# One common table in place of two: where the two attention phases of a decoder and recurrence kernel put their matrix products

## The reference, cut to what matters

```python
def attention(q, k, v, mask):                       # 16 heads of 32 channels
    scores = einsum('bhqd,bhkd->bhqk', q, k) / sqrt(32)
    scores = scores * mask - 10000.0 * (1.0 - mask)
    probs = softmax(scores, axis=-1)
    return einsum('bhqk,bhkd->bhqd', probs, v)

qkv = layernorm(hidden, ln1_s, ln1_b) @ w_qkv + b_qkv          # self attention
x = hidden + merge(attention(split(q), split(k), split(v), ltor_mask)) @ w_ao + b_ao
q = layernorm(x, ln2_s, ln2_b) @ w_q + b_q                     # cross attention
k, v = split2(encoder @ w_kv + b_kv)
x = x + merge(attention(split(q), split(k), split(v), cross_mask)) @ w_co + b_co
x = x + gelu(layernorm(x, ln3_s, ln3_b) @ w1 + b1) @ w2 + b2   # then the recurrent layer
```

## Time and profile before

| | us |
|---|---|
| median of 3 runs | 4188.12 |
| lowest and highest | 4186.58, 4194.16 |
| the profiled execution | 4188.12 |
| its span, first to last instruction | 4186.3 |
| scores of the self phase, first to last | 48.8 to 756.9 |
| scores of the cross phase, first to last | 824.6 to 1555.9 |

### The profile page before, as it was taken

One profiled execution on the slowest core, in us unless ns is written; L12 is line 12 of the kernel. 1 busy time (PEld: TensorE's weight loads), 2 busy tenths in 40 slices (PEclk: granted clock), 3 DMA queues, 4 the chain that ended last, 5 costly groups with the idle time before them and its releaser, 6 DMA issues. The chain is left out here.

```text
span 4186.3 us, 71343 instructions
## 1 busy us (share of the span) xinstructions
PE 3717.9 (89%) x21636; PEld 2881.0 (69%) x21636; DVE 2995.5 (72%) x6732; ACT 2059.3 (49%) x5384; POOL 1732.2 (41%) x1210
## 2 busy tenths in 40 slices
PE   5999999589999986999999678999999999999976
PEld 4877777477777765999999555666666666666633
DVE  5777777488888865655655258878787878788872
ACT  5777777477777765545554312333333333333322
POOL 2444444144444440000000136666666666666652
PEclk9999999799999998999999899999999999999988
DMA  3444443344444433001001201000000000000000
GB/s 112 106 105 105 105 110 95 114 116 115 120 126 112 115 93 118 30 30 45 30 30 35 106 14 29 23 23 24 23 22 20 23 24 24 24 24 24 23 18 15
DMA packets 146612, 256.58 MB, mean 61 GB/s; under 512 B 27185, under 2 KB 32049, under 8 KB 145425
## 3 DMA queue, kind: packets, MB, share of 16 engines
q1 hardware_dynamic: 146448, 254.49, 22.1%
HBM read 107.62 MB, written 33.55 MB: 34 GB/s over the span
## 5 line engine op out<-in xcount | busy, mean ns | idle before, releaser
L1204 POOL TENSOR_TENSOR c_S<-c_S,c_rT 128x1024 f32<-128x1024 f32 x256 | 558.0, 2180 | 459.4 <-DVE c_S L1482 418.3
L1482 DVE TENSOR_TENSOR_SCAN c_S<-c_wT,c_s,c_vb 128x256 f32<-128x256 f32 x1024 | 708.7, 734 | 45.0 <-issue 2.7
L1477 DVE TENSOR_TENSOR c_vb<-c_kT,c_vb 128x512 f32<-128x512 f32 x512 | 352.1, 688 | 286.9 <-PE c_vb L1648 255.6
L351 POOL TENSOR_TENSOR x_prob<-x_prob,x_rsums 128x512 f32<-128x512 f32 x256 | 269.5, 1055 | 429.5 <-DVE x_rsums L513 429.5
L351 POOL TENSOR_TENSOR s_prob<-s_prob,s_rsums 128x512 f32<-128x512 f32 x256 | 269.3, 1055 | 415.7 <-DVE s_rsums L513 415.7
L1648 PE MATMUL c_vb<-c_vhl,c_spread 128*128 128x512 f32 x512 | 300.3, 596 | 73.8 <-DVE c_S L1482 60.6
L407 ACT ACTIVATE s_prob<-s_t,s_tmin 128x256 f32<-128x256 f32 x512 | 256.4, 502 | 183.6 <-DVE s_tmin L506 182.3
L407 ACT ACTIVATE x_prob<-x_t,x_tmin 128x256 f32<-128x256 f32 x512 | 256.2, 501 | 181.6 <-DVE x_tmin L506 180.9
L865 PE MATMUL b_ps<-b_ln_high,b_w_high 128*128 128x256 f32 x1024 | 290.8, 284 | 15.0 <-DVE b_ln_low L807 15.0
L866 PE MATMUL b_ps<-b_ln_low,b_w_high 128*128 128x256 f32 x1024 | 290.7, 284 | 0.0
L867 PE MATMUL b_ps<-b_ln_high,b_w_low 128*128 128x256 f32 x1024 | 290.6, 284 | 0.0
(11 more groups left out here) (266 smaller groups left out, 10632.4 us busy)
## 6 DMA issues: line engine op xcount, KB each, us to landing
s_stack<-s_parts_qk SPq DMA_DIRECT2D x384, 128.0 KB, 2.4
x_stack<-x_parts_qk SPq DMA_DIRECT2D x384, 128.0 KB, 2.4
s_x_in<-in_x SPq DMA_DIRECT2D x16, 512.0 KB, 3.5
s_xb<-in_x SPq DMA_DIRECT2D x16, 512.0 KB, 4.0
x<-s_x_out SPq DMA_DIRECT2D x16, 512.0 KB, 4.7
x_enc<-in_ctx SPq DMA_DIRECT2D x16, 512.0 KB, 4.4
x_x_in<-x SPq DMA_DIRECT2D x16, 512.0 KB, 3.7
x_xb<-x SPq DMA_DIRECT2D x16, 512.0 KB, 4.2
```

The source lines that it names most:

```text
L351: nc.gpsimd.tensor_tensor(prob[:, h % 4, :, :], prob[:, h % 4, :, :], rsums[:, h, :].unsqueeze(2).to_broadcast([P, TC, T]), ALU.mult).then ...
L1204: nc.gpsimd.tensor_tensor(S[:, n % 4, :, 0:T], S[:, n % 4, :, 0:T], rT[:, par, :, :], ALU.mult).then_inc(z_ready, 1)
L1477: nc.vector.tensor_tensor(pair(vb, i), pair(kT[:, par, :, :], i), pair(vb, i), ALU.mult)
L1482: op = nc.vector.tensor_tensor_scan(S[:, n % 4, c, 1:T + 1], wT[:, par, c, :], vb[:, c, :], s0[:, par, c, n:n + 1], ALU.mult, ALU.add)
```

## The change

The two tables of fills and the two tables of slots are replaced by one table for both phases, in which slot 6 gets `encT0` and `encT1` in the cross phase, and by fixed slots: `xb` in slot 1, statistics in slot 4, root in slot 5, application in slot 6. What is computed stays the same, instruction for instruction, within the loop. Side by side:

| slot | self before | cross before | both after |
|---|---|---|---|
| 0 | ctx2 | q3 | k2, ctx2 |
| 1 | | k2 | q3 |
| 2 | q3 | k3 | k3 |
| 3 | k3, k2, ctx3 | ctx2 | |
| 4 | | ctx3, v0 | ctx3 |
| 5 | v0 | v1 | v0 |
| 6 | v1 | out0, encT0 | v1 (and encT0, encT1 in cross) |
| 7 | out0, lnT0, lnT1 | lnT0, lnT1 | lnT0, lnT1, out0 |
| 8 | out1 | encT1 | out1, ctx0 |
| 9 | ctx0, q0 | out1, q0 | q0 |
| 10 | k0 | k0 | k0 |
| 11 | q1, k1 | ctx0, q1 | q1 |
| 12 | q2 | k1 | k1, ctx1 |
| 13 | ctx1 | q2 | |
| 14 | | ctx1 | |
| 15 | | | q2 |

```diff
-    SELF_FILLS = {0: ["ctx2"], 2: ["q3"], 3: ["k3", "k2", "ctx3"], 5: ["v0"], 6: ["v1"], 7: ["out0", "lnT0", "lnT1"], 8: ["out1"], 9: ["ctx0", "q0"], 10: ["k0"], 11: ["q1", "k1"], 12: ["q2"], 13: ["ctx1"]}
-    SELF_AT = {"xb": 2, "root": 3, "stats": 3, "apply": 6}
...
-    CROSS_AT = {"xb": 1, "root": 4, "stats": 4, "apply": 6}
...
+    FILLS = {0: ["k2", "ctx2"], 1: ["q3"], 2: ["k3"], 4: ["ctx3"], 5: ["v0"],
+             6: ["v1"] + (["encT0", "encT1"] if cross else []), 7: ["lnT0", "lnT1", "out0"], 8: ["out1", "ctx0"],
+             9: ["q0"], 10: ["k0"], 11: ["q1"], 12: ["k1", "ctx1"], 15: ["q2"]}
...
-                        if n == AT["xb"] and "lag" in parts:
+                        if n == 1 and "lag" in parts:
...
-                        if n == AT["root"] and "front" in parts:
+                        if n == 5 and "front" in parts:
...
-                        if n == AT["stats"] and "front" in parts:
+                        if n == 4 and "front" in parts:
...
-                        if n == AT["apply"] and "front" in parts:
+                        if n == 6 and "front" in parts:
```

More of the change, by code:

```diff
@@ L131, in attention_phase @@
     LT = 3
-    SELF_FILLS = {0: ["ctx2"], 2: ["q3"], 3: ["k3", "k2", "ctx3"], 5: ["v0"], 6: ["v1"], 7: ["out0", "lnT0", "lnT1"], 8: ["out1"], 9: ["ctx0", "q0"], 10: ["k0"], 11: ["q1", "k1"], 12: ["q2"], 13: ["ctx1"]}
-    SELF_AT = {"xb": 2, "root": 3, "stats": 3, "apply": 6}
-    CROSS_FILLS = {0: ["q3"], 1: ["k2"], 2: ["k3"], 3: ["ctx2"], 4: ["ctx3", "v0"], 5: ["v1"], 6: ["out0", "encT0"], 7: ["lnT0", "lnT1"], 8: ["encT1"], 9: ["out1", "q0"], 10: ["k0"], 11: ["ctx0", "q1"], 12: ["k1"], 13: ["q2"], 14: ["ctx1"]}
-    CROSS_AT = {"xb": 1, "root": 4, "stats": 4, "apply": 6}
-    FILLS, AT = (CROSS_FILLS, CROSS_AT) if cross else (SELF_FILLS, SELF_AT)
+    FILLS = {0: ["k2", "ctx2"], 1: ["q3"], 2: ["k3"], 4: ["ctx3"], 5: ["v0"],
+             6: ["v1"] + (["encT0", "encT1"] if cross else []), 7: ["lnT0", "lnT1", "out0"], 8: ["out1", "ctx0"],
+             9: ["q0"], 10: ["k0"], 11: ["q1"], 12: ["k1", "ctx1"], 15: ["q2"]}
     PART = {"attn": ("k2", "q3", "k3", "v0", "v1", "ctx0", "ctx1"), "lag": ("ctx2", "ctx3", "out0", "out1"),
```

## The result

| | before | after |
|---|---|---|
| median, us | 4191.14 (4 runs) | 4256.09 (4 runs) |
| lowest and highest | 4186.58, 4195.77 | 4250.41, 4262.61 |
| the profiled execution | 4188.12 | 4252.74 |
| its span | 4186.3 | 4250.9 |

The changed kernel takes 1.0164 times as long, 95% interval 1.0145 to 1.0182: slower by 65 us, where 50 were forecast. The ratio rests on all 14 executions of the kernel after, whose median is 4259.7 us; the four in the table are among them.

A forecast was written before the change was run, and what follows sets the result against it. PE was busiest (94%, 91%), its work unchanged, so only waits could change. Needed work plus waits gave 45.2 us (self) and 48.8 (cross); taking 0.8 and 2.5 more, 15 x 3.3 = 49.5 on 4188.12: 4238 us, range 4193 to 4282.

The forecast's parts named there:

- The main step: End of a pass, both phases: DVE waits for ACT's high part of q2, so head 0's t_ready comes about 2.4 us late.
- The price of the end of a pass: From head 13's scores, S(13), to the next pass's S(0): 6.8 us with 3.5 of PE work, so 3.3 lost, both phases.
- The start of a cross pass: Cross, slots 2 to 5: waits at head 2's scores and the transposes T(2) to T(5), together 4.3 us a pass.
- the 39.4 of needed work: PE's work in a cross pass, priced from instruction starts: 39.4 us, unchanged by the table; 38.5 in self.
- overlap lost at the restarts: PE, after each wait: 0.4 us a pass added for overlap lost at each restart, in self and cross.
- The encoder's bank: Cross, slot 7: out0 must wait for encT0's low part, 1.35 us a pass lost; lnT's 0.9 waits go.
- Self: Self pass: 38.5 + 3.3 + 3.0 + 0.4 = 45.2 us, 0.95 over 44.25; taken as 0.8 for uncertain slow clock.
- ctx2's bank: Self, start of a pass: ctx2 takes the bank q2 had and waits for its low part, 0.5 us.
- The rival in which the clock decides for the worse: Both phases: 3.4 us of PE work a pass at 1.2 GHz, 1.7 us more a pass, 4289 us; chance 0.13.
- No change: Both phases: PE's work is the same and it is busiest, so waits only change places, 4188 us; chance 0.09.
- faster: Shorter runs of light slots lose less: self gains 2 us a pass, cross loses 0.5, 4166 us; chance 0.11.

The follow-up runs named there:

- the late move: Kernel after, with only DVE's part of q2's move taken in slot 1 of the next pass, PE's and ACT's order kept: 4214.09 us, 1.0052.
- the edit that took away one wait of 1.04 us: Kernel after, with slot 7 filled as out0, lnT0, lnT1 instead of lnT0, lnT1, out0: 4228.84 us, 1.0077.
- three edits with xb in slot 2: Kernel after, with DVE's move of q2 a slot later, out0 first in slot 7, ctx2 in slot 3, and xb in slot 2: 4163.27 us, 0.9932.
- the same edit was worth 8 us: ctx2 in slot 3 instead of 0: on the kernel after 4247.89 us; with q2's DVE move a slot later and out0 first too, 4148.82.
- two experiments: Kernel after, with POOL's sum of xb in slot 5 instead of slot 1, then in slot 6: 4311.06 us, 1.0287, and 4315.58 us, 1.0291.

## Why the prediction came out as it did

**The main step held: q2 in slot 15 makes DVE wait, and head 0 is late.** The walk put DVE's head 0 at S(13) + 10.95, with a wait of some 2 us for ACT's high part; in the rows it is at 1238.18 - 1227.36 = 10.82, behind a wait of 1.93. Taking only that step of DVE out of the way gave back 42 us, and q2 in slot 15 of the kernel before cost 85: the entry is shown from both sides, and the late move, which leaves PE's order alone, shows the mechanism.

**The price of the end of a pass held; of its cause I saw only one half.** I wrote S(0) = S(13) + 6.8 by the chain from k1's low part over SP's issue to the stack. The median over the passes is 6.57, in both phases, and in 9 of 14 passes of each that chain is what ends the wait. In the pass from 1030.92 on SP issues at S(13) + 2.76 and S(0) follows 3.78 later, where I took 3.79. What the forecast left out are the transposes of slots 14 and 15, which follow the exponentials of heads 12 and 13. With no fill beside them T(14) and T(15) waited 0.48 and 1.19 us (medians) for ACT, and q2 filled the rest but for 0.5 us. So of the idle time that I put ahead of S(0) most stands ahead of the transposes. In the other 5 passes q2 runs at the half clock, and S(0) comes at S(13) + 6.8 to 7.35. The two chains end within half a microsecond of each other, so the sum did not notice; taking one away shows the other, as q2 in slot 14 did (1.95 us at S(0), which itself did not move).

**The start of a cross pass** went as walked: T(2) at S(13) + 14.1 by forecast and 14.15 in the rows, S(3) at 16.0 and 16.05, T(3) at 17.1 and 17.0. The losses that I wrote beside them are larger than PE's idle time there (medians per slot: T(2) 1.4 against 1.18, T(3) 0.9 and 0.56, T(4) 1.1 and 0.93, T(5) 0.5 and 0.27, S(2) 0.4 and 0.21; 4.3 against 3.15). The same holds for the whole pass: 9.4 us over the 39.4 of needed work forecast and measured, of which the trace shows 5.95 as idle. A pass before has 6.8 over it, 4.03 of them idle. What was counted from start to start is the loss; idle rows show some two thirds of it. A part of the rest is slow clock: 27.3 us at half clock in 14 cross passes are, by my estimate, at most 1 us a pass (half of 27.3/14). What is left I can only call overlap lost at the restarts, which the forecast put at 0.4 a pass; no run measures it apart. (The edit that took away one wait of 1.04 us gave 1.26.)

**The encoder's bank.** Forecast 1.35 a pass, measured 1.04; the edit that removes it gives 1.26 in cross. The same edit gives self 0.48, since lnT ahead of out0 makes PE wait for x there; the forecast had this at nothing.

**Self.** Forecast 45.2, measured 45.37 to 45.67. Idle T(2) 0.38, T(3) 0.56, T(4) 0.93, T(5) 0.27, and 2.18 at the end; ctx2's bank, forecast at 0.5, cost nothing that shows. What kept self from growing as cross did is PE's busy time, and the clock goes with it, though no run holds the two apart: self had 61.5 us at half clock in its 14 passes before, 17.1 after. I said that this could get better or worse and took 0.15 us a pass off; busy time fell by 0.64. Why it rose by 0.75 in cross at the same clock stays open. The rival in which the clock decides for the worse did not happen: 27.3 us in cross against 23.8. I had read one cross pass with a full clock at its start; it is so in every second pass only, 7 of the 14 have the half clock there. And after, the half clock fell on q2, not on k2, ctx2 and q3 as I had written. The Trainium skill ("TensorE: Matmul & The Clock Gate", section "HAM oscillation — how this bites in real kernels") ties such stretches to a wait in each round. The traces agree in where they stand (behind 1.19 us at T(15), behind 1.95 us at S(0) with q2 in slot 14), and differ in how often: after, 5 of 14 self passes have one, though each has the wait.

**What the sum missed.** Of the 15 us between the 49.5 forecast and the 64.6 of the spans, 7 are the passes (57 instead of 49.5 us), as self grew by 1.12 instead of 0.8 and cross by 2.67 instead of 2.5. The others lie ahead of, between and behind the passes counted, where the forecast had nothing. Part of that need not be an effect of the change: DVE's first work on the weights is 1.4 us later in that execution, and in the traces of the edited kernels the first head comes anywhere from 48.7 to 51.7 us. The rest I have not taken apart.

**No change and faster** fell as their conditions fell: S(0) came at 6.57, not after 9, and PE's waits were not fixed, since PE was the busiest engine in all of these kernels while its idle time per pass, by slot medians, went from 2.11 us (self, three edits with xb in slot 2) over 6.36 (cross, after) to 7.69 (cross, xb in slot 6).

## What to carry to other kernels

In a loop whose engines work in order, the last slot is also what stands ahead of the next round: a move that is taken in the slot of its own fill puts everything behind it late; taken one slot into the next round it held up little here (0.36 us a pass in self). Give light slots a fill each, and judge a fill's place only once the largest wait is gone: the same edit was worth 8 us before that and 37 after. Before a chain is priced, walk every consumer in it, since two chains that end together hide one another.

## What the runs showed of the hardware

Beside an instruction of POOL some of DVE's operations on SBUF last until POOL's has ended, and others don't notice it. With POOL's addition (2.39 us, all operands in SBUF) a tensor_scalar of 128x2 took 1.91 us instead of 0.17, and one of 128x512 up to 2.55 instead of 0.54. Beside POOL's scaling the mask's copy took 1.23 instead of 0.43, and the subtraction of lnT's low part, which has two inputs in SBUF, up to 1.54 instead of 0.67:

```profile
L462 DVE TENSOR_TENSOR x_ln_low<-x_lnT,x_ln_high x32: 669/693/1540, 830.8 to 1556.5; 128x512 fp32r<-128x512 f32 x32
```

The layernorm's statistics (L105 0.67, L108 0.17) and the reciprocal (L510 0.16), with one input in SBUF too, keep their times beside POOL, and so do the operations that read PSUM (L485 0.48, L499 0.70). The long tensor_scalars reversed the sign of two experiments. The Trainium skill ("GPSIMD Engine Reference", section "1. Specifications") says that the two engines share their SBUF interfaces, with contention in a two-port mode or with two SBUF inputs. The trace agrees for the two inputs; it does not say which operations run in a two-port mode. The price in each case is about what is left of POOL's instruction.

Where the half clock falls is as fragile: q2's fill moved by one slot took it from q2 (5 of 14 cross passes, S(0) 0.7 us later) to k2 and ctx2 (12 of 14, slot 0 longer by 1.5 us), while the waits ahead of it were 1.19 us in one case and 1.95 in the other.
